# Thought stage of a fused transformer kernel: normalisation applied behind the first product, the thought summed by TensorE as rows and as columns, loads waited for by user

## What is computed

```python
x_norm = layer_norm(x, in_gamma, in_beta)             # x: already normalised once
thought = x_norm[:, -1, :] @ agg_w + agg_b            # 4 rows of 256, one of each sequence
for _ in range(4):
    t = layer_norm(thought, pn_gamma, pn_beta)
    t = gelu(t @ d1_w + d1_b)                         # 256 -> 1024
    thought = thought + (t @ d2_w + d2_b)             # 1024 -> 256
broadcast = (thought @ bc_w + bc_b)[:, None, :]
gate = sigmoid(x @ gate_w + gate_b)
out = x + gate * broadcast
return layer_norm(out, out_gamma, out_beta)
```

## Time and profile before

| what | value |
|---|---|
| median of 3 runs | 2220.29 us (2219.08 to 2224.95) |
| the profiled execution: span, first to last instruction | 2224.5 us, 43127 instructions |
| the profiled execution's own time | not given apart from the span; 2224.5 us is taken for it |
| TensorE busy / VectorE / ScalarE / GpSimd | 90% / 67% / 52% / 31% of the span |
| TensorE's granted clock, mean | 0.940 of full speed |
| thought stage | 835.8 us to 918.0 us of the span |

### The profile page before, as it was taken

One profiled execution on the slowest core, in us unless ns is written; L12 is line 12 of the kernel. 1 busy time (PEld: TensorE's weight loads), 2 busy tenths in 40 slices (PEclk: granted clock), 3 DMA queues, 4 the chain that ended last, 5 costly groups with the idle time before them and its releaser, 6 DMA issues. The chain is left out here.

```text
span 2224.5 us, 43127 instructions
## 1 busy us (share of the span) xinstructions
PE 1997.6 (90%) x13031; PEld 1713.8 (77%) x13031; DVE 1498.0 (67%) x4236; ACT 1156.4 (52%) x2628; POOL 681.9 (31%) x1298
## 2 busy tenths in 40 slices
PE   5688796999999995799999884999879999987998
PEld 3444475779999992599999773999769999976887
DVE  6578576847787884788888771422278888875665
ACT  3656442847676661466666411444346666653333
POOL 3312201103334321233333155544323333312221
PEclk9889898999999996899999887999989999988999
DMA  2066502012122104430000023999820000014331
GB/s 66 9 115 154 169 18 71 1 48 79 52 78 71 58 20 155 159 110 0 0 0 0 28 92 117 316 315 318 271 81 16 21 21 14 14 31 121 116 112 41
DMA packets 145258, 193.66 MB, mean 87 GB/s; under 512 B 45084, under 2 KB 113285, under 8 KB 142217
## 3 DMA queue, kind: packets, MB, share of 16 engines
q1 hardware_dynamic: 121096, 153.51, 23.0%
q0 software_dynamic: 7632, 20.85, 2.5%
q10 hardware_dynamic: 16400, 17.70, 2.4%
HBM read 169.86 MB, written 56.62 MB: 102 GB/s over the span
## 5 line engine op out<-in xcount | busy, mean ns | idle before, releaser
L2613 DVE COPY l2f_x_t<-bank 128x256 f32<-128x256 f32 x111 | 47.1, 425 | 152.4 <-PE bank L2336 149.4
L2478 POOL DMA_INDIRECT l2f_y_rows<-l2f_y,l2f_target x111 | 112.0, 1009 | 121.8 <-ACT l2f_y L2446 119.4
L724 ACT ACTIVATE l1a_prob<-l1a_masked,l1a_shift,l1a_q_scale 128x512 f32<-128x512 f32 x128 | 104.5, 817 | 76.4 <-DVE l1a_shift L782 74.7
L724 ACT ACTIVATE l2a_prob<-l2a_masked,l2a_shift 128x512 f32<-128x512 f32 x128 | 92.7, 725 | 79.0 <-DVE l2a_shift L786 76.2
L724 ACT ACTIVATE l3a_prob<-l3a_masked,l3a_shift 128x512 f32<-128x512 f32 x128 | 92.7, 725 | 78.1 <-DVE l3a_shift L786 75.2
L2348 PE MATMUL bank<-l2f_x_t,l2f_w 128*128 128x128 f32 x888 | 117.4, 275 | 0.4 <-DVE l2f_x_t L2613 0.4
L1297 ACT ACTIVATE l0a_prob_t<-bank 128x512 f32<-128x512 f32 x128 | 76.2, 599 | 64.8 <-PE bank L1235 64.0
L2348 PEld LDWEIGHTS bank<-l2f_x_t,l2f_w 128*128 128x128 f32 x888 | 108.0, 192 | 0.7 <-issue 0.6
L1314 DVE TENSOR_REDUCE l0a_coarse<-bank 128x32 f32<-128x512 f32 x128 | 87.5, 688 | 26.5 <-PE bank L1225 24.7
L776 DVE CUSTOM_DVE_ANT_0 l3a_masked<-bank,l3a_side 128x512 f32<-128x512 f32 x128 | 88.4, 691 | 14.2 <-issue 12.9
L776 DVE CUSTOM_DVE_ANT_0 l2a_masked<-bank,l2a_side 128x512 f32<-128x512 f32 x128 | 88.4, 691 | 12.6 <-issue 10.8
(11 more groups left out here) (603 smaller groups left out, 7467.7 us busy)
## 6 DMA issues: line engine op xcount, KB each, us to landing
l2f_w<-w_rows SPq DMA_DIRECT2D x111, 304.0 KB
l1a_side<-rms SPq DMA_DIRECT2D x16, 1024.0 KB, 4.8
l2f_x_rows_of<-x_slots ACTq DMA_DIRECT2D x111, 128.0 KB
w_rows<-in_l2f_w SPq DMA_DIRECT2D x4, 2048.0 KB
l2f_hots<-l2f_y_rows SPq DMA_DIRECT2D x8, 768.0 KB, 10.0
l3f_raw<-in_l3f_w SPq DMA_DIRECT2D x24, 256.0 KB, 3.8
l3f_mix<-shares SPq DMA_DIRECT2D x16, 384.0 KB, 3.7
l2f_w_rest<-in_l2f_w SPq DMA_DIRECT2D x111, 48.0 KB
```

What stands on the lines that cost most here:

```text
L724: act.activation(prob[:, unit, :], masked[:, unit, :], ACT.Exp, bias=shift[:, unit:unit + 1], scale=q_scale[:, slot, t:t + 1] if qk_norm e ...
L2478: pool.indirect_dma_start(y_rows, bass.IndirectOffsetOnAxis(target[:, b:b + 1], 0), y[:, b % of.Y_SLOTS, :], None).then_inc(y_stored[b % o ...
L2613: dve.tensor_copy(x_t[:, b % 2, :], turn_bank[b % 2][:, 0:D]).then_inc(x_kept, 1)
```

## The change

Six edits, all in `thought_stage` and its two helpers:

1. **Loads waited for by user.** The one semaphore becomes seven groups. SyncE issues `agg_w`, `d1_w`, `gate_w`, `d2_w`, `bc_w`, each with its bias, in order of use; nine small loads move to ScalarE's queue (L1935 to L1941). GELU's table is loaded by a dummy activation behind them (L1942).
2. **First rows.** The two normalisations in a row become one, by `rstd = ((1 + eps) * var + EPS * eps) ** -0.5`.
3. **The thought is kept in PSUM twice**, as columns (256 features on partitions, 32 rows: 8 copies of the 4) and as rows on all 128 partitions. A product with the identity puts `thought + d2_b` into each bank, and the step's result is added to it by TensorE.
4. **Normalisation behind the first product.** The columns times gamma go straight into the product with `d1_w`; then `hidden = (product - mean * sums) * rstd + offsets`, with `sums = gamma @ d1_w` and `offsets = beta @ d1_w + d1_b` computed once. Mean and variance are taken from the rows while TensorE multiplies.
5. **Gate products move** from behind the step's sum to behind its first product, and one head product each joins them in steps 3 and 4 (`BEHIND`).
6. **The end.** The thought's columns are spread to 128 rows per sequence by VectorE (`batch_t`) and multiplied by `bc_w`, with the bias as a product of K=1; four banks, ScalarE copies three of them, VectorE takes the gates of two tiles and GpSimd six.

```diff
+    BEHIND = (0, 0, 1, 1)
@@ SyncE @@
-                for n, name in enumerate(small_names):
-                    sp.dma_start(small[:, n, :], dram[name].partition_broadcast(B)).then_inc(first_loaded, 16)
+                load("agg_w", agg_loaded)
...
+                load("d1_w", d1_loaded)
+                load("gate_w", gate_loaded)
...
+                load("d2_w", d2_loaded)
...
+                load("bc_w", out_loaded)
@@ GpSimd @@
-                for t in range(TT):
+                for t in range(2, TT):
                     pool.wait_ge(gate_done, t + 1)
+                    pool.wait_ge(said_kept, t * B // TT)
@@ TensorE @@
+                pe.wait_ge(d1_loaded, 96)
                 pe.transpose(active_bank[0:chunks, 0:P], d1_columns[:], m.ident[:]).then_inc(bias_turned, 1)
                 norm.tensor(pe)
-                pe.wait_ge(loaded, 16 * n_loads)
                 for n in range(STEPS1):
-                    turn(1 + n)
...
+                    pe.wait_ge(rows_set, n + 2)
+                    past_rows(hidden_bank, lambda c: rows_t[:, c, :]).then_inc(hidden_ready, 1)
...
+                    gate_products(step_tiles(n))
+                    for h in range(sum(BEHIND[:n]), sum(BEHIND[:n + 1])):
+                        products.tensor(pe, h)
                     pe.wait_ge(active_done, n + 1)
...
+                    pe.matmul(columns, m.ident[:], ahead_t[:].rearrange("p c r -> p (c r)"), start=True, stop=False)
+                    if n + 1 < STEPS1:
+                        pe.wait_ge(rows_kept, n + 1)
+                        pe.matmul(thought, m.ident[:], ahead[:], start=True, stop=False)
...
                     pe.wait_ge(parts_kept, n + 1)
-                    pe.matmul(row_bank[0:B, 0:D], sum_of[:], parts[:], start=True, stop=True).then_inc(product_ready, 1)
-                    gate_products(step_tiles(n))
+                    for to in range(DC):
+                        last = pe.matmul(columns[:, to * ROWS:(to + 1) * ROWS], parts[:, to * P:(to + 1) * P], sum_of[:],
+                                         start=False, stop=(to == DC - 1))
+                    last.then_inc(thought_ready, 1)
+                    if n + 1 < STEPS1:
+                        pe.matmul(thought, sum_all[:].rearrange("p g r -> p (g r)"), parts[:], start=False,
+                                  stop=True).then_inc(rows_ready, 1)
@@ VectorE, one step @@
+                        turn_thought(n)
+                        measure_thought(n)
                     dve.wait_ge(hidden_ready, n + 1)
-                    dve.tensor_tensor(hidden[:], hidden_bank[:, 0:span], d1_b[:], ALU.add).then_inc(hidden_set, 1)
+                    link(dve.scalar_tensor_tensor(centred[:], minus_sums[:], moments[:, 0:1], hidden_bank[:, 0:span], ALU.mult, ALU.add))
+                    dve.wait_ge(rstd_done, n + 1)
+                    dve.scalar_tensor_tensor(hidden[:], centred[:], rstd[:], offsets[:], ALU.mult, ALU.add).then_inc(hidden_set, 1)
```

More of the change, by code:

```diff
@@ L1817, in gate_products @@
                         last.then_inc(gate_ready, 1)
-                pe.wait_ge(first_loaded, 16 * n_first)
-                turn(0)
-                project(weights["agg_w"])
+                pe.wait_ge(rows_set, 1)
+                for c in range(DC):
+                    last = pe.transpose(active_bank[:, c * B:(c + 1) * B], rows[:, c * P:(c + 1) * P], m.ident[0:B, 0:B])
+                last.then_inc(turned, 1)
+                pe.wait_ge(agg_loaded, 48)
+                pe.wait_ge(set_up, 2)
@@ new lines, in _ @@
+                pe.matmul(columns, bias_columns[:], to_chunk[:].rearrange("c g r -> c (g r)"), start=True, stop=False)
+                pe.matmul(thought, ones_row[:], bias_rows[:], start=True, stop=False)
+                pe.wait_ge(turn_kept, 1)
+                for to in range(DC):
+                    for c in range(DC):
+                        last = pe.matmul(columns[:, to * ROWS:(to + 1) * ROWS], weights["agg_w"][:, c, to * P:(to + 1) * P],
+                                         first_t[:, c, :], start=False, stop=(to == DC - 1 and c == DC - 1))
@@ L1863, in _ @@
+                for b in range(B):
+                    if b >= 2:
+                        pe.matmul(said_of(b), ones_row[:], bc_b[:], start=True, stop=False)
+                    pe.wait_ge(batch_set, b + 1)
+                    for c in range(DC):
+                        last = pe.matmul(said_of(b), batch_t[:, b, c, :], weights["bc_w"][:, c, :], start=False, stop=(c == DC - 1))
+                    last.then_inc(said_ready, 1)
+                for h in range(sum(BEHIND), HEADS):
                     products.tensor(pe, h)
@@ L1880, in _ @@
+                act.wait_ge(offsets_ready, 1)
+                act.copy(offsets[:], active_bank[:, 0:span]).then_inc(offsets_kept, 1)
                 for n in range(STEPS1):
[L1881 to L1885 removed]
@@ new lines, in _ @@
+                link(dve.tensor_scalar(rows[:], last_x[:], moments[0:B, 0:1], rstd[0:B], ALU.subtract, ALU.mult))
+                dve.wait_ge(affine_loaded, 32)
+                link(dve.tensor_tensor(rows[:], rows[:], in_affine[:, 0, :], ALU.mult))
+                dve.tensor_tensor(rows[:], rows[:], in_affine[:, 1, :], ALU.add).then_inc(rows_set, 1)
+                norm.take_moments(dve, 1)
+                dve.wait_ge(set_up, 5)
+                turn_thought(0)
+                measure_thought(0)
```

358 lines of the change are left out of this document (197 added, 161 removed).

## The result

The changed kernel takes **2208.61 us** (median of 5 runs, 2206.23 to 2213.47) against 2220.29 for the kernel before (5 runs, 2218.26 to 2224.95). The ratio is 0.9945, 95% interval 0.9931 to 0.9960: 12 us or 0.55% faster. A second comparison on another chip gave 2208.8 against 2217.94, ratio 0.9961, 0.9947 to 0.9974. The forecast was 2202.2, so the sign and the range were right; the gain was two thirds of what I had worked out, and by the second comparison (9 us) half.

The account below looks back on a forecast made before the run. The thought stage was taken as one serial chain of 82.2 us, 3.7% of the span, with no engine full in its steps. Gains of 5.1 + 7.0 + 6.0 = 18.1 us gave 2202.2 us, range 2195.5 to 2213.

Parts of the forecast that it names:

- Part 1: Thought stage from its start to the end of step 1, 27.9 us before: gain 5.1 us, bounds 2.6 to 8.
- The clock before step 1: TensorE behind the tile transposes: full clock expected in step 1; by the skill's rule 1.2 GHz and a gain of 2.6 us.
- Part 2: Steps 2 to 4 of the thought stage, 30.95 us before: 24.0 us expected, gain 7.0, between 11.6 and -2.2.
- the middle case: Steps 2 to 4 take 24.0 us, a third of the way from full-clock 19.3 to half-clock 33.1; chance 0.48.
- Part 3: End of the thought stage behind step 4, 23.35 us before: gain 6.0 us, bounds 3 and 7.5.
- Heads start at 2.9: End of the stage: 14 head products start about 2.9 us behind the last sum and end at 16.8.
- The stage of 64 us: Sign of being right: the whole thought stage, 82.2 us before, lasts about 64 us.
- a tail over 20 us: Sign of being wrong: the tail at the thought stage's end lasts over 20 us.
- Three steps in 24 us: Sign of being right: steps 2 to 4 take 24 us with TensorE's clock over 0.8.
- the end does not shrink: Rival, stage's end: GpSimd still sets the pace, VectorE's shared reads are slower; end gains 2 us, total 2206.2; chance 0.06.
- Warm all through: Rival, steps 2 to 4 at full clock: they gain 11.6 us, 22.7 in all, 2197.6 us; chance 0.25.
- The slower case: Rival, stage's start: small loads served behind `d1_w` land about 866, 21 us late; 3 us slower, 2223.2; chance 0.04.

Follow-up runs that it names:

- the second profile: The changed kernel run again unaltered in the second comparison, against the kernel before: 2208.8 us, ratio 0.9961.
- the third: Third profile of the changed kernel, run again unaltered on a chip where the kernel before took 2227.32 us: 2221.65 us, one run.
- the norms first: Changed kernel with the eight tiles' norm and transposes put ahead of ScalarE's copy of `pn` and VectorE's `turn_thought(0)`: 2210.79 us.
- the dense bias: Changed kernel with the end's K=1 bias products made K=128, `bc_b` broadcast to 128 rows: 2202.32 us, ratio 0.9932 to the kernel before.

## Why the prediction was right, and where it was not

**Part 1**, predicted gain 5.1, measured 2.0 and in the kernel's other profiles up to 3.1 (24.8). The chain was the right one; its terms add up 2.8 us short (861.39 instead of 858.6; the stage began 0.3 earlier, so the part is 3.1 longer). First copy 842.74 instead of 842.0. The 8 records of 32 columns took 1.92 and not 1.2: I had priced them by number instead of noting that each loads new weights of 128 columns. The transposes therefore began 1.5 us late and took 0.5 more. The three passes, bias and offsets took 4.3 (852.74 to 857.03) instead of 3.3, for ScalarE's two copies (`minus_sums`, `offsets`) and four 8-row products lie between them. The drain of about 1.4 us that the Trainium skill's "ScalarE: Activation LUTs", section "What ACT_TABLE_LOAD costs", adds to a table load did not show: the load ended at 842.61, the activation began at 842.63 and the next copy at 842.74. Nor did it ahead of the sigmoids' load: ScalarE's copy ended at 880.54, the load began at 880.56, and the first sigmoid at 881.85.

**The clock before step 1.** The windows of the earlier trace rows made me expect full clock behind the transposes. In the first profile all 16 ran at half, and the clock rose 0.6 us into the first pass over `d1_w`:

```profile
850.30:853.30 3.00, 2.75 (x17) 0.50 1.07 357
853.30:856.30 3.00, 3.00 (x52) 1.00 1.12 341
```

So the 16 records took 1.32 us instead of 1.07 and the passes behind them ran at full clock. Of the 3.1 us missing, the half clock made 0.25 there and the 0.5 of the transposes, which in the kernel before ran at full clock at their end. In the second profile the clock rose a microsecond before the last transposes ended (855.6, transposes to 856.6), in the third 2.1 us into the first pass, and with the norms first 6.0 us behind the last transpose. The rule of the Trainium skill's "TensorE: Matmul & The Clock Gate", section "Part 4: PE-mode transpose", that transposes do not count as busy, fits the first, the third and the norms first; the second and the kernel before, where the clock rose 2.9 us into the transposes, speak against it. Its gain of 2.6 us is nearer to the 2.0 measured than my 5.1, but by luck: it has step 1 at 1.2 GHz, and all but the first 0.6 us of it ran at 2.4.

**Part 2**, predicted gain 7.0, measured 9.5: the middle case was too careful. The clock was 1.00 through steps 2 to 4, and so it was in every other profile but the one in which TensorE waits for the reciprocal. My full-clock step was 6.0 us and the measured one 6.44. Two terms carry it. The sum in columns was to save 0.3 of the old sum's 0.6, but released VectorE after 0.67 (860.72 to 861.39): moving an eighth of the columns saved nothing. And from hidden to the second product it is 2.1 instead of 2.0. The reciprocal and `centred` end together (869.80 and 869.85), so `hidden` starts 2.07 us behind the sum, 2.15 predicted. A head added 0.88 instead of 0.65.

**Part 3 is the step that failed**: predicted gain 6.0, measured -0.7 in the first profile. "Heads start at 2.9" is wrong at any clock: the 16 records of `bc_w` and two pairs of bias records stand ahead of them, 4.90 at 2.4 GHz with the dense bias. I had taken the time of GpSimd's first gate for that of the first head. With 4.90 the last copy ends at S + 18.4 and part 3 gains 5. The other 5 to 6 us are the clock, for which part 3 of the prediction had no term. The sum assumed 2.4 GHz there without saying so. Without the spell the same kernel's part 3 takes 19.5 us, a gain of 4.2. Yet the trace of the kernel before had the warning, in windows that I had not asked for, behind its own products with few rows (the spread with `pick`, 4 partitions):

```profile
897.60:900.60 3.00, 2.50 (x12) 1.00 0.01 3
900.60:903.60 3.00, 3.00 (x14) 0.63 0.00 0
903.60:906.60 3.00, 3.00 (x18) 0.80 0.00 0
```

**The signs named.** The stage of 64 us was 71.7 in the first profile, and 65.7 and 66.9 in two others. One sign of being wrong came true in the first profile: a tail over 20 us (24.3). No wait for `out_beta`: right. Three steps in 24 us: 21.4. VectorE's tail and the last head copy within 1 us of each other: 4.4 apart with the spell, 1.6 without. Of the rivals, "the end does not shrink" came true in the first profile, though not by its mechanism (GpSimd's pace) and not in the other two, where the end shrank by 4.2: its 2206.2 is nearer to the result than my forecast, which is luck. That the result lies in the range is in part luck too: part 2 gave 2.5 us more than forecast while part 1 gave 3.1 less, and the 6.7 us missing in part 3 had no case of their own. "Warm all through" was right for the steps. The slower case, small loads served behind the big ones, did not come: the last of those that the first product waits for landed by 845.8.

**What stays open.** In the changed kernel's profiles without the spell the stage gains 15.6 to 16.8 us, near the 18.1 predicted, yet the medians differ by 12 and 9. Part of the answer lies ahead of the stage. In those two profiles it began 4.4 and 4.0 us later than in the kernel before (835.79), and with the spell 0.3 earlier, so that its *end* comes at 907.2, 905.9 and 906.7 in the three, against 918.3: 11.2 to 12.5 us earlier in each, close to the 12 us of the first comparison. Why the late start and the missing spell go together is open. So is whether the kernel before also has executions that begin near 840, and what its stage takes then: it has one profile.

## To carry to other kernels

Work that is moved out of a serial chain into its shadow pays at full clock: running the product beside the statistics gave 1.7 us a step, and moving independent products behind it 0.7 to 1.6. When the terms of a sum are TensorE's durations, ask for each stretch at which clock they hold, and query the granted clock of the stretch before as well as the one the change touches. A bias by a product with one row costs little in records (0.8 us here without the spell), but behind a serial chain it did not keep the clock up, in four profiles of six; a dense operand with zeros does the same work and held the clock in all six. And before a stage's gain in a profile is set against the medians, look at when the stage began: here that alone differed by 4.7 us between two executions of the same kernel.

## What was not expected of the hardware

- With K=1 products (1x256) behind the last step, TensorE was granted 0.50 for up to 10 us although it was busy 3.00 of 3.00 us in the windows; a pair took 1.22 us there. A pair of 128x256 in the same place took 0.59 and the clock stayed at 1.00.
- The same kernel showed a stage of 71.7, 65.7 and 66.9 us in three profiles, the first two at nearly the same span (2206.8 and 2205.9): the longest began 4.7 and 4.3 us earlier than the other two, and all three ended within 1.3 us of each other.
- Two issues of 128 rows of 4 bytes (`d2_b`) held ScalarE's queue for 2.44 us, where the four of the same form just before them (`pn`) took 2.05 together.
- ScalarE ran on at once behind a table load (0.02 us).
